# Experts two at a time, 64 tokens each in the two column halves of the array

## The reference

```python
scores = jax.nn.sigmoid(xt @ Wg.T + bg)          # 1250 x 64
w, idx = jax.lax.top_k(scores, 2)
w = w / w.sum(-1, keepdims=True)
cw = jnp.zeros((T, E)).at[jnp.arange(T)[:, None], idx].add(w)
nx = (xt - mu) * jax.lax.rsqrt(var + EPS)
h1 = einsum('td,edh->eth', nx, gamma[:, :, None] * W1) + b1p[:, None, :]
h3 = einsum('td,edh->eth', nx, gamma[:, :, None] * W3) + b3p[:, None, :]
h = jax.nn.silu(h1) * h3
y = einsum('eth,ehd->td', h * cw.T[:, :, None], W2) + cw @ b2
z = shared expert(nx * gs + bs)                  # Ws1, Ws3, Ws2, all tokens
return y + z
```

## Time and profile before

| | |
|---|---|
| median of three executions | 1034.34 us (1029.65 to 1034.5) |
| span of the profiled execution | 1036.3 us |
| PE busy | 822.9 us (79%) |
| PE weight loads busy | 579.7 us (56%) |
| DVE / ACT / POOL busy | 567.5 / 318.9 / 471.7 us |
| DMA traffic | 189.12 MB, mean 182 GB/s |
| up, L1005 | 237.7 us busy, 2048 passes |
| down, L1012 | 120.5 us busy, 256 passes |

### The profile page before, as it was taken

One profiled execution on the slowest core, in us unless ns is written; L12 is line 12 of the kernel. 1 busy time (PEld: TensorE's weight loads), 2 busy tenths in 40 slices (PEclk: granted clock), 3 DMA queues, 4 the chain that ended last, 5 costly groups with the idle time before them and its releaser, 6 DMA issues.

```text
span 1036.3 us, 17634 instructions
## 1 busy us (share of the span) xinstructions
PE 822.9 (79%) x5020; PEld 579.7 (56%) x5020; DVE 567.5 (55%) x1449; ACT 318.9 (31%) x872; POOL 471.7 (46%) x638
## 2 busy tenths in 40 slices
PE   0979885146987888774429999999999999999980
PEld 0966553123544444442227577677777777777750
DVE  4878898825966656568895744322322232222225
ACT  0244442057255545553046121121112122111110
POOL 2415444875277777768250032343334444434420
PEclk9667898567989888898656999999999999999995
DMA  5324354385366575753102025688888878888837
GB/s 169 84 56 102 96 125 137 89 235 156 104 175 223 163 226 163 238 165 89 61 21 82 1 85 192 211 276 294 289 280 292 295 276 285 284 299 289 290 108 297
DMA packets 79880, 189.12 MB, mean 182 GB/s; under 512 B 19286, under 2 KB 20491, under 8 KB 79840
## 3 DMA queue, kind: packets, MB, share of 16 engines
q1 hardware_dynamic: 54356, 128.50, 37.3%
q0 software_dynamic: 22272, 56.42, 18.3%
q10 hardware_dynamic: 3212, 3.70, 1.1%
HBM read 180.78 MB, written 18.41 MB: 192 GB/s over the span
## 4 chain that ended last, share of the span: by engine, by line
issue 23%; PE 21%; POOL 12%; DMA 11%; DVE 9%; DVEq 2%; another core or an unknown queue 1%; POOLq 1%; ACT 0%
PE ps L888 14%; DMA y_rows<-xn,stage_s 9%; POOL xn L512 5%; POOL y_rows L517 4%; PE ps L891 3%; POOL spare L447 2%; DMA ring<-y_rows 2%; PE ps L941 1%; DVE ring L1289 1%; DVE stats L1337 1%; DVE acc L1334 1%; DVE S L1285 1%; DVE x_sb L1334 1%; PE ps L927 1%
## 5 line engine op out<-in xcount | busy, mean ns | idle before, releaser
L1005 PEld LDWEIGHTS ps<-xn,arena 128*128 128x128 f32 x2048 | 236.0, 192 | 42.1 <-issue 28.6
L1005 PE MATMUL ps<-xn,arena 128*128 128x80 f32 x2048 | 237.7, 274 | 4.7 <-DVE xn L1507 2.9
L888 PE MATMUL ps<-ring,S 128*128 128x512 f32 x320 | 183.9, 703 | 69.7 <-DVE ring L1289 42.7
L1507 DVE TENSOR_SCALAR xn<-ps,arena 128x80 f32<-128x80 f32 x256 | 74.6, 354 | 254.0 <-PE ps L773 234.1
L470 POOL DMA_INDIRECT ring<-h_rows,idx_stage x160 | 176.5, 1103 | 44.1 <-issue 40.3
L631 ACT ACTIVATE ring<-ring,p_c 128x64 f32<-128x64 f32 x480 | 130.3, 337 | 131.3 <-DMA ring<-h_rows,idx_stage 98.1
L888 PEld LDWEIGHTS ps<-ring,S 128*128 128x128 f32 x320 | 63.0, 219 | 118.7 <-issue 59.8
L447 POOL TENSOR_TENSOR spare<-iota_p 128x1 f32<-128x1 f32 x200 | 41.5, 211 | 175.7 <-ACT xn L715 124.7
L1012 PE MATMUL ps<-arena,acc 128*80 128x512 f32 x256 | 120.5, 593 | 0.8 <-ACT xn L715 0.8
L1285 DVE TENSOR_SCALAR S<-iota_row,dloc 128x128 f32<-128x128 f32 x176 | 63.5, 361 | 84.8 <-remote 45.5
L715 ACT COPY xn<-ps 80x512 f32<-80x512 f32 x64 | 37.2, 581 | 207.5 <-PE ps L1012 177.5
(11 more groups left out here) (268 smaller groups left out, 950.8 us busy)
## 6 DMA issues: line engine op xcount, KB each, us to landing
arena<-in_L_ffn_W_dram SPq DMA_DIRECT2D x192, 512.0 KB
arena<-edge_keys SPq DMA_DIRECT2D x20, 320.0 KB
ring<-y_rows SPq DMA_DIRECT2D x9, 512.0 KB, 6.2
ring<-edge_keys SPq DMA_DIRECT2D x10, 320.0 KB
h_rows<-ring SPq DMA_DIRECT2D x10, 256.0 KB, 4.5
ring<-h_rows,idx_stage POOLq DMA_INDIRECT x160
nx_rows<-xn SPq DMA_DIRECT2D x10, 256.0 KB, 2.0
x_sb<-in_x_dram SPq DMA_DIRECT2D x3, 768.0 KB
```

Source lines behind the costliest of these rows:

```text
L888: pe.matmul(ps[:, j % 4, :], S[:, k % 4, :], rows[:, k, :], start=(u == 0), stop=(u == 1))
L1005: o = pe.matmul(ps[:, bank + 2 * w, m * TS:(m + 1) * TS], w13[:, u, w, a, m * P:(m + 1) * P], xgT[:, k, a, :], start=(a == 0), stop=(a == ...
L1507: o = v.tensor_scalar(xgT[:, k, a, :], ps[:, bank, a * TS:(a + 1) * TS], gT[:, 0, a, e], gT[:, 1, a, e], ALU.mult, ALU.add)
```

## The change

`TOKENS` becomes 64, and experts are worked off in pairs (`NPAIR` = 32). A tile of 128 places holds expert 2j in places 0 to 63 and expert 2j+1 in 64 to 127; `slot_tab` has one column a pair. One gather, one set of four 128x128 transposes, one scatter serve the pair.

- `up`: the tokens are stationary, 64 columns of an expert at a time, and the weights are streamed, 512 columns (W1 beside W3). The output stands with the tokens on the partitions: expert 2j in partitions 0 to 63, expert 2j+1 in 64 to 127 of the same bank. The matmuls of the two alternate, eight a pair. The bias is now along the free dimension, and is added by one more matmul over all 128 columns: a selection matrix (`choose`, DVE) by the table of biases.
- `hidden_turn`: two new transposes a pair, since the hidden values must be turned before `down`, and a copy of them on DVE (`hidden_T`).
- `down`: four matmuls a pair, 64 hidden columns stationary, W2 streamed.
- `scale_in` is two DVE operations of 512 columns in place of eight of 80 a pair.
- Weights: three buffers of a pair each (six experts; the third lies where the edge tables were), W1 and W3 reloaded after `up` and W2 after `down`, rows of 4 KB for all three. All loops over pairs are written out.
- POOL: the copies of indices and the `settle` operations are gone from the loop; the gather of pair j+2 is issued after pair j is turned, ahead of the scatter of pair j. There are two token buffers.
- The first two pairs are loaded at work items 32 and 64 of the graph layer, the third after the last item.
- Places within a pair's tile take a handful of small DVE operations more in the router. An expert with more than 64 tokens has its rest in an overflow tile, which is worked off at the end.

```diff
-TOKENS = 80
+TOKENS = 64
-            for u in range(U):
-                sp.wait_ge(s("pe_item"), 2 * IB * (u + 1))
-                load_expert(u, bass.ds(u, 1))
+            for j in range(2):
+                sp.wait_ge(s("pe_item"), 4 * IB * (j + 1))
+                load_up(j)
+                load_down(j)
...
-            with sp.Fori(1, NIT) as i:
-                for u in range(U):
-                    sp.wait_ge(s("pe_y"), U * (i - 1) + u + 1)
-                    load_expert(u, bass.ds(U * i + u, 1))
+            for j in range(WB, NPAIR):
+                sp.wait_ge(s("pe_up"), j - WB + 1)
+                load_up(j)
+                sp.wait_ge(s("pe_y"), j - WB + 1)
+                load_down(j)
...
+            gather(0, slots(0, 0), xg_landed[0])
+            gather(1, slots(1, 0), xg_landed[1])
+            for j in range(NPAIR):
+                if j + 2 <= NPAIR:
+                    pool.wait_ge(s("pe_xgT"), j + 1)
+                    gather(j % 2, slots(j + 2, 0), xg_landed[j % 2])
+                pool.wait_ge(s("y_ready"), j + 1)
+                scatter(j % 2, slots(j, 1), y_out[j % 2])
...
-            def up(u, k, bank, done1, done3):
-                for w, done in ((0, done1), (1, done3)):
-                    for m in range(M):
-                        for a in range(A):
-                            o = pe.matmul(ps[:, bank + 2 * w, m * TS:(m + 1) * TS], w13[:, u, w, a, m * P:(m + 1) * P],
-                                          xgT[:, k, a, :], start=(a == 0), stop=(a == A - 1))
+            def up(k, b, halves, done):
+
+                pe.matmul(ps[:, 2 + k, :], sel[:, k, :], bb1[:, :], start=True, stop=False, skip_group_check=True)
+                for a in range(A):
+                    for x in range(halves):
+                        c = slice(TS * x, TS * x + TS)
+                        o = pe.matmul(ps[c, 2 + k, :], xgT[:, k, a, c], w13[b][:, x, :, a, :],
+                                      start=False, stop=(a == A - 1), skip_group_check=True)
+                o.then_inc(s(done), 1)
+
+            def hidden_turn(k, rows, done):
                 for m in range(M):
-                    o = pe.matmul(ps[0:TS, bank, :], hT[:, k, m, :], w2s[:, u, m, :], start=(m == 0), stop=(m == M - 1))
+                    o = T(ps[:, 4, m * P:m * P + rows], hm[0:rows, k, m::M], rows)
                 o.then_inc(s(done), 1)
+            def down(k, b, halves, done):
+                for m in range(M):
+                    for x in range(halves):
+                        c = slice(TS * x, TS * x + TS)
+                        o = pe.matmul(ps[c, 5 + k, :], hT[:, k, m, c], w2s[b][:, x, m, :], start=(m == 0), stop=(m == M - 1))
+                o.then_inc(s(done), 1)
...
+            for j in range(NPAIR + 1):
+                if j < NPAIR:
+                    pe.wait_ge(w13_landed[j % WB], 32 * (j // WB + 1))
+                    pe.wait_ge(s("xgT_done"), j + 1)
...
+                    up(j % 2, j % WB, 2, "pe_up")
+                    if j + 1 < NPAIR:
+                        pe.wait_ge(xg_landed[(j + 1) % 2], 16 * ((j + 1) // 2 + 1))
+                        turn((j + 1) % 2, "pe_xgT")
+                if j >= 1:
+                    pe.wait_ge(s("hT_done"), j)
+                    pe.wait_ge(w2_landed[(j - 1) % WB], 16 * ((j - 1) // WB + 1))
...
+                    down((j - 1) % 2, (j - 1) % WB, 2, "pe_y")
+                if j in BESIDE:
+                    aside(j)
...
+                if j < NPAIR:
+                    pe.wait_ge(s("hm_done"), j + 1)
...
+                    hidden_turn(j % 2, P, "pe_hT")
```

## The result

The changed kernel takes 1053.45 us (median of four executions, 1046.8 to 1060.45) beside 1031.99 us (four, 1024.15 to 1034.5) for the kernel before: a ratio of 1.0206, 95% interval [1.0138, 1.0273]. It is slower, by some 2%, and not faster by 3.5% as forecast. What bounds it is the ring of the prediction's rival 2, in which the gather of a later pair stands behind the scatter of a finished one. That the measured time lies near rival 2's 1059 us is in part luck: the rival came to it with a landing of 7.8 us at full clock, the trace has 6.3 us and a lower clock.

The account below looks back on a forecast made before the run. PE was taken to bound the expert stage, with DMA close behind. From the profiled 1036.3: stage -59, overflow tile +19, router +1, graph layer +3 give 1000, less 2.0 makes 998 us; range 945 to 1078.

Parts of the forecast that it names:

- the ring: Expert stage: down, copy, scatter, gather, transposes, next down; 10.0 us, taken as 10.5 us a pair with DMA's limit.
- rival 2: Ring of gather and scatter sets the pace: 12.9 us a pair, 1059 us, slower; decides from 11.9 us on; chance 0.12.
- The landing: Gather's time from issue until landed: taken as 5 us, against 3.0 with DMA nearly idle and 5.9 median for loaded scatters.
- Transposes and down: PE's members of the ring: 0.6 us and 1.9 us; at half clock 2.4 us more, priced in rival 2 only.
- The stage: Expert stage: seven pairs at 11.0, 25 at 10.5, plus 5 us, is 344 against 403, so -59 us.
- The first seven pairs: Start of the expert stage, with the shared expert's rest, 21 us in all: taken as 11.0 us a pair.
- Halves side by side: Up and down on PE: passes into output partitions 0 to 63 and 64 to 127 run at the same time, 5.2 us.
- rival 1: Up and down's halves run one after the other: about 12.1 us a pair with waits, 1075 us, slower; chance 0.20.
- What PE needs in a pair: Bias, up, down and six transposes on PE: 6.7 us side by side, some 8.5 with imperfect pairing.
- DMA: Weights plus gathers and scatters, 3.47 MB a pair at 350 GB/s: 9.9 us a pair.
- Overflow tile: One tile after the last pair, for expert 1's 76 tokens: +19 us, with 13 and 28 as ends.
- Graph layer and router: Before the experts: router operations +1 us (0 to 3), waits stretched by weight loads +3 us (-4 to +8).

Follow-up runs that it names:

- experiment 1: Changed kernel with the scatter of pair j-2, in place of pair j, behind the gather of pair j+2: 927.19 us, ratio to the kernel before 0.9003.
- experiment 9: Changed kernel, but SP asks for w2 of a pair, and the weights behind it, only when that pair's gather has landed: 1006.08 us.
- experiment 2: Changed kernel with three unused float32 matmuls of 512 columns between up and the wait for the gather, from pair 8 on: 1016.93 us.
- experiment 4: Changed kernel with the scatter of pair j-2 behind the gather of pair j+2, and only half of the weights loaded from the fourth pair on: 910.94 us.
- experiment 5: Changed kernel with the scatter two pairs later and up's matmuls half by half, four lower then four upper, in place of alternating: 975.41 us.
- experiments 1 and 10: The second of these: changed kernel with the scatter of pair j-1 behind the gather of pair j+2: 929.88 us, ratio to the kernel before 0.9085.
- experiment 8: Changed kernel with the scatter two pairs later and the overflow tile's weights asked for one pair earlier: 929.02 us, ratio to the kernel before 0.9019.
- experiment 3: Changed kernel, but from the fourth pair on only the first expert of a pair has its weights loaded: 991.41 us.

## Why the prediction was wrong

The step that failed is the ring: "with a landing of 5 us, nearer to the loaded scatter since the queues will be fuller, it is 10.0", and from it 10.5 us a pair. The ring was there, with the members the prediction listed; two of its terms were mis-sized, and it was given too small a chance.

- *The landing*, taken as 5, is 6.3. It was taken from a range, as if the gather met an average load. DMA is busy 65% of the stage, but the ring issues every gather into its full part, the burst that the same down released; a full DMA alone makes it near 6 us, as experiment 1 shows, and experiment 9, which moves the burst, makes it 4.8. This puts the prediction's ring at 10.0 + 1.3 = 11.3. The steps between down's end and the gather's issue, taken as 2.4 us, are 2.8, so 11.7, which is what experiment 2 has at full clock.
- *Transposes and down*, taken as 0.6 + 1.9, are 4.73 at the lower clock. The prediction priced it ("at half clock the ring's down and transposes take 2.4 us more") but in the rival only. The two belong together: a ring longer than PE's work gives PE idle time, and that makes the ring longer. 11.7 + 2.2 = 13.9, and 13.8 stands in the trace. Experiment 2 took this second part away alone.
- *The argument against the rival*, "a fuller DMA queue means that PE is fed", mixed two things. The queue was full of weights for a later pair, while PE waited for a small transfer behind them.

The stage came out at 407 for the forecast's 344, 63 us, while the whole missed by 55. The first seven pairs took 82.8 us for 77. From pair 8 to 30 the pairs are 13.5 us apart for 10.5; as an estimate, the landing makes 1.3 of these 3.0, the steps behind down 0.4, the clock 1.6 (13.5 less the 11.9 of experiment 2 in the mean) and what else lengthens experiment 2's mean 0.2, less the 0.5 that the prediction had put on top of its ring.

The other steps:

- *Halves side by side*: right. Up's 16 passes take 3.65 us, where one file would be 6.9, and rival 1 falls. The Trainium skill (TensorE: Matmul & The Clock Gate, Part 3, Packing small matmuls) says that matmuls in different column groups run concurrently; the trace agrees, for float32 in two halves of 64 columns.
- *What PE needs in a pair*: 6.7 taken, 7.43 measured (experiment 4). Full-width passes to half-width ones start 788.67 - 787.72 = 0.95 us after two turns of 0.43, as this row of experiment 5 shows, and 3.58 us lie between up and the transposes in experiment 1 where 8 turns are 3.44. The four transposes take 0.68 us until down starts, where the prediction's 0.11 each are 0.44. All in all the pair is 0.73 us longer than taken, 0.18 for each of its four changes.

```profile
787.72 1.02 PE L985 MATMUL ps<-arena,xn 128*128 128x512 f32 x2
788.67 5.42 PE L989 MATMUL ps<-edge,xn 128*64 128x512 f32 x16
```

The Trainium skill (TensorEngine Tiling (Array Packing), Tiling Modes) says that a change of the tiling mode drains the array. The trace agrees in that time is lost at each change; on what, it doesn't show. The 0.16 us a change that the prediction tried for this rule was near, though its rows 4 have no such gap; it was hidden here as foreseen.

- *DMA*: 9.9 us a pair taken (350 GB/s), and it would have been 8.6: experiments 1 and 10 move a pair at 406 to 408 GB/s for 150 us, with PE beside it. The prediction's reason for less, that only an end without other work showed 407, doesn't hold. That the kernel before had 363 GB/s at a share of 0.99 may come from its smaller packets (128.50 MB in 54356 packets of the weights' queue q1, now 130.07 MB in 45060); no run shows it. This error was hidden by the ring.
- *Overflow tile*: +19 taken, +17 measured; it took its weights 3.2 us late, and experiment 8 shows that they weren't the only thing late.
- *Graph layer and router*: +4 taken, +2 seen, which is less than that layer varies between executions (the stage of these kernels starts between 592 and 605 us).
- *Rival 1's sum*: its 29 us of shared work don't follow from the 21 us that the prediction counts for the first seven pairs; with 21 it is 1067 and not 1075 us, still slower.
- *The chances*: 0.12 for rival 2 was too low, as the ring at the prediction's own loaded landings (5.9 median) and lower clock comes to 10.9 + 2.4 = 13.3, above its point of decision, 11.9.

In sum: pairing is worth 105 us (1032 to 927), the overflow tile's 17 already taken off, and the ring costs 126 (927 to 1053).

## What to carry to other kernels

When a buffer count is cut, write down every chain that runs from one iteration's result through a queue to the next iteration's input, and put its length at the moment where each link starts: a small transfer that is released by the same event as a large one landed behind it here, and a small one behind a queue that is always full as late. If the ring is longer than TensorE's work, add what it costs at the lower clock at once, not as a separate risk. In an in-order queue, put the issue that the next iteration needs ahead of the one that finishes the last; one place of slack was as good as two. Whether a third token buffer would give the same slack was not tried.

## What the runs showed of the hardware

- Passes into different column halves overlap although they stand in one queue, and not only with their neighbours: 16 passes take 3.65 us alternating, 5.42 with eight and eight, and 8 passes 1.94 with four and four.
- The granted clock fell from 1.00 to 0.50 with PE idle for 3.65 us ahead of 865.55, and stood at 0.50 through 4 us of unbroken work (852 to 856). Useless passes in that gap kept it up in most pairs and made the expert stage 32 us shorter (experiment 2).
- A gather of 128 places, 78 of them real rows of 2 KB in the mean (2500 picks in 32 pairs), lands in 2.6 us at best (experiments 3 and 9) and in 6.3 in the middle when 3.1 MB are asked for 2 us ahead of it. With DMA full throughout one took near 6 us (experiment 1), and one landed about 2 us after the weights ran dry (experiment 9). Why half of the burst took 6 us and not 3.8 in the turn shown in experiment 3 stays open.
